# Attention stage of a ViT layer: router matmuls inside the second score train, wide weights in two buffers, q expanded by ScalarE, values split around the second heads

## The reference, cut to what matters

```python
# 64 images of 36 tokens, width 192; 12 heads of 16; 8 experts, 2 chosen; inner width 768
h = patches(x) @ W.T + b
q, k, v = split(h @ w_qkv)
a = softmax((q @ k.T * SCALE) * (1 - temperature * eye(n)))
h = layernorm(h + (a @ v) @ w_proj + b_proj)
scores = sqrt(softplus(h @ gate_w))               # router, top 2 of scores + gate_bias
expert = lambda x, W1, W2, W3: (silu(min(x @ W1, 10)) * clip(x @ W3, -10, 10)) @ W2
h = layernorm(h + expert(h, w1s, w2s, w3s) + sum over the two chosen e of weight_e * expert(h, w1[e], w2[e], w3[e]))
```

## Time and profile before

| | |
|---|---|
| median of 3 runs | 707.46 us (705.86 to 707.53) |
| profiled execution | 701.57 us, of which the span shown is 699.8 us |
| mean granted TensorE clock | 0.897 of full speed |
| PE busy | 607.3 us (87%) |
| DVE, ACT, POOL busy | 467.0, 330.9, 209.1 us |
| first group's scores read by DVE | at 30.78 us |
| last group's | at 246.79 us |

### The profile page before, as it was taken

How to read it: one execution, slowest core, us unless ns; L and a number is a source line. 1 busy time by engine, 2 the same in 40 slices (tenths; PEclk the granted TensorE clock), 3 DMA queues, 4 the chain that set the end, 5 groups by cost and what they waited for, 6 DMA issues and landing times.

```text
span 699.8 us, 15524 instructions
## 1 busy us (share of the span) xinstructions
PE 607.3 (87%) x4542; PEld 468.0 (67%) x4543; DVE 467.0 (67%) x1072; ACT 330.9 (47%) x596; POOL 209.1 (30%) x215
## 2 busy tenths in 40 slices
PE   4979999998999978884278999999999999999981
PEld 2767778686787866553146777777777777777761
DVE  0376887878768795772358766666666666667785
ACT  1456654656637553741123444444444444445434
POOL 1123444243433442337720022222222212122232
PEclk9999988799959756997569999999999999999995
DMA  7152534435350532522210111111111111111612
GB/s 273 57 175 65 163 94 142 137 99 162 117 163 14 163 97 48 166 60 77 71 46 19 24 40 40 40 40 40 40 39 37 35 39 36 40 40 39 206 32 101
DMA packets 56680, 57.97 MB, mean 83 GB/s; under 512 B 22817, under 2 KB 52785, under 8 KB 55377
## 3 DMA queue, kind: packets, MB, share of 16 engines
q1 hardware_dynamic: 52752, 49.63, 24.3%
q0 software_dynamic: 3904, 8.06, 3.4%
HBM read 41.83 MB, written 15.83 MB: 82 GB/s over the span
## 4 chain that ended last, share of the span: by engine, by line
PE 69%; DVE 12%; issue 6%; another core or an unknown queue 5%; ACT 4%; POOL 1%; DMA 1%; ACTq 0%; SPq 0%; DVEq 0%; POOLq 0%
PE bank L679 25%; PE bank L700 12%; PE bank L689 6%; PE bank L540 6%; PE bank L525 4%; PE bank L551 3%; PE bank L598 3%; PE bank L610 2%; PE bank L580 2%; PE bank L667 2%; PE bank L563 1%; DMA con<-consts 1%; PE bank L613 1%; DVE arena L980 1%
## 5 line engine op out<-in xcount | busy, mean ns | idle before, releaser
L679 PE MATMUL bank<-W,arena 128*128 (+1 forms) x1220 | 214.1, 331 | 6.2 <-issue 6.2
L679 PEld LDWEIGHTS bank<-W,arena 128*128 128x128 f16 x1220 | 121.1, 99 | 82.1 <-issue 12.3
L700 PE MATMUL bank<-W,arena 128*128 (+1 forms) x1098 | 106.9, 254 | 20.9 <-issue 11.7
L700 PEld LDWEIGHTS bank<-W,arena 128*128 128x128 f16 x1098 | 96.6, 101 | 31.0 <-issue 13.2
L1509 POOL DMA_INDIRECT ybuf<-arena,slot x43 | 41.9, 974 | 217.9 <-ACT arena L898 213.1
L1183 DVE SCALAR_TENSOR_TENSOR arena<-bank,sct,arena 128x384 f16<-128x384 f32 x86 | 49.1, 613 | 73.1 <-ACT arena L890 73.1
L525 PE MATMUL bank<-arena,par 128*96 128x288 f32 x192 | 64.0, 427 | 10.5 <-DMA con<-consts 10.0
L1197 DVE SCALAR_TENSOR_TENSOR arena<-arena 128x384 f32<-128x384 f32 x122 | 69.4, 569 | 4.2
L689 PE MATMUL bank<-con,arena 128*128 128x128 f32 x366 | 55.8, 288 | 17.1 <-issue 14.4
L884 ACT ACTIVATE arena<-bank,sct 128x384 f32<-128x384 f32 x86 | 50.0, 581 | 42.9 <-PE bank L679 41.6
L1192 DVE TENSOR_SCALAR arena<-bank,sct 128x384 f32<-128x384 f32 x86 | 58.2, 677 | 9.1 <-PE bank L679 8.9
(11 more groups left out here) (156 smaller groups left out, 898.5 us busy)
## 6 DMA issues: line engine op xcount, KB each, us to landing
stage<-w_all SPq DMA_DIRECT2D x9, 1344.0 KB, 6.0
arena<-xT SPq DMA_DIRECT2D x8, 864.0 KB, 4.6
stage<-w_all SPq DMA_DIRECT2D x9, 768.0 KB, 5.0
arena<-dbuf SPq DMA_DIRECT2D x43, 96.0 KB
dbuf<-arena SPq DMA_DIRECT2D x6, 679.0 KB, 7.1
W<-ybuf SPq DMA_DIRECT2D x3, 1152.0 KB, 8.2
xbuf<-arena SPq DMA_DIRECT2D x8, 216.0 KB, 2.3
arena<-xbuf SPq DMA_DIRECT2D x3, 576.0 KB, 5.8
```

What stands on the lines that cost most here:

```text
L679: m = pe.matmul(bank[2 * k + n][:, 0:I // 2], xT16[:, b, lo, tail, :], W16[:, bass.ds(off + at + col, I // 2)], start=(z == 0), stop=(z == ...
L700: m = pe.matmul(bank[6][:, 0:C], hhT[:, lo, ic, :], W16[:, bass.ds(off + at + ic * C, C)], start=(ic == 0 and z == 0), stop=(ic == IC - 1 ...
```

## The change

- PE: the three router tiles, two matmuls each, stand after the 4th, 5th and 7th score matmul of the second train; their logits lie in another PSUM bank, so the wait for `s_lgr` moves from ahead of `probsT(g, 0)` to ahead of `heads(g, 0)`. `project(g+1, 1)` moves ahead of `probsT(g, 1)`. The values are split: one half ahead of `heads(g, 1)`, the other behind.
- ACT: q is expanded by six ACT instructions, not two of DVE. `h1T_out` and the first half of `hT_out` stand ahead of the first exponential; the tail's `weights_hi` stands ahead of the second.
- DVE: it normalises the second half itself, behind its own `sums`. `weights_lo_tail` is moved ahead of nine steps of the choice, `weights_lo_main` behind the second `heads_out`.
- SP: `main` goes in turn to `stage` and to the unused part of `W16` that later holds the last expert; it is loaded two groups ahead, the tail one group ahead.

```diff
+        mains = stage[:, MAIN:STW], W16[:, E * WF:(E + 1) * WF].bitcast(F32)[:, 0:UPW + DNW]
+        logits = bank[4][0:TM, 440:440 + GTILES * E]
+        ROUTER_AFTER = (4, 5, 7)
...
                 wait_apart(sp, s_wlo, g * 2 + 1)
-                load_main(g + 1)
-                if tail:
+                load_tail(g + 1)
+                if main:
                     wait_apart(sp, s_wlo, g * 2 + 2)
-                    load_tail(g + 1)
+                    load_main(g + 2, odd)
...
+                        if routing and n in ROUTER_AFTER:
+                            router_tile(g - 1, ROUTER_AFTER.index(n), logits, g * 2 + 1)
...
-                scores(g, 1, None if last else embed(g + 1, 1))
-                if not start:
-                    router(g - 1)
-                    pe.wait_ge(s_lgr, g)
+                scores(g, 1, None if last else embed(g + 1, 1), routing=not start)
                 probsT(g, 0)
                 if not last:
                     project(g + 1, 0)
                 heads(g, 0)
+                if not last:
+                    project(g + 1, 1)
                 probsT(g, 1)
                 if not last:
-                    project(g + 1, 1)
+                    values(g + 1, (0,))
                 heads(g, 1)
                 if not last:
-                    values(g + 1)
+                    values(g + 1, (1,))
...
+            def q_out(g):
+                for tp in range(2):
+                    act.wait_ge(s_qk, g * 4 + 1 + tp)
+                    for hh in range(HH):
+                        m = AC.activation(qblk[:, tp].rearrange("p b (h n) -> p h b n", h=HH)[:, hh],
+                                          bank[tp][0:RT, 0:GT].rearrange("p (b n) -> p b n", b=G), ACT.Copy,
+                                          scale=K("qmask")[0:RT, hh:hh + 1])
+                    m.then_inc(s_q, 1)
...
                 if not start:
                     h1T_out(g - 1)
-                weights_hi(g, (0,))
                 if not last:
-                    hT_out(g + 1)
+                    hT_out(g + 1, (0,))
+                exps(g, 0)
+                weights_hi(g, odd, (0,))
+                if not last:
+                    hT_out(g + 1, (1,))
                 if not start:
                     logits_out(g - 1)
+                weights_hi(g, odd, (1,))
                 exps(g, 1)
                 probsT_out(g, 0)
+                if not last:
+                    q_out(g + 1)
                 if not start:
                     softplus_ln(g - 1)
-                weights_hi(g, (1,))
                 probsT_out(g, 1)
...
                 sums(g, 1)
-                weights_lo_main(g)
-                between(2)
+                normalise(g, 1)
                 heads_out(g, 0)
-                between()
-                if not last:
-                    q_out(g + 1)
-                between(2)
                 weights_lo_tail(g)
-                between(4)
+                between(9)
                 heads_out(g, 1)
+                weights_lo_main(g, odd)
                 if last:
                     x_lo(0, 0)
                 norm(g, between)
...
                 if i == COUNT_AT + 2:
-                    weights_lo_main(E)
+                    weights_lo_tail(E)
                 elif i == COUNT_AT + 3:
-                    weights_lo_tail(E)
+                    weights_lo_main(E, 0)
```

More of the change, by code:

```diff
@@ L446, in _ @@
             load_x(XT, 1)
-            group(GROUPS - 1, load=False, store=False, choice=False, tail=False)
+            group(GROUPS - 1, 1, load=False, store=False, choice=False, main=False)
             def load_h1(q):
@@ L542, in project, with values @@
                     m.then_inc(s_qk, 1)
-            def values(g):
-                pe.wait_ge(s_q, g * 2 + 2)
-                for half in range(2):
+            def values(g, halves=(0, 1)):
+                if 0 in halves:
+                    pe.wait_ge(s_q, g * 2 + 2)
+                for half in halves:
                     for pair in range(2):
@@ L761, in _ @@
             X(1, 1)
-            router(GROUPS - 1, 4)
+            for t in range(GTILES):
+                router_tile(GROUPS - 1, t, logits_last, None)
             pe.wait_ge(s_lgr, GROUPS)
```

144 lines of the change are left out of this document (77 added, 67 removed).

## The result

| us | before | after |
|---|---|---|
| median of 4 runs | 706.66 (703.14 to 707.53) | 686.80 (685.51 to 688.14) |
| profiled execution | 701.57 | 688.09 |
| its span | 699.8 | 686.3 |

The ratio is 0.9717 (95% interval 0.9662 to 0.9773): faster by 19.9 us, where 8.2 were forecast. 686.8 lies 12.5 under the forecast and 0.2 under its range.

The account below looks back on a forecast made before the run. PE, busy 87% of the span, was taken as the bound. Groups -23.3, last group +3.0, after them +1.2, falls +10.9 took 701.57 to 693.4 profiled; 5.9 more for the median gave 699.3 us, range 687 to 712.

Parts of the forecast that it names:

- the term +10.9: Seven groups: the clock falls in three of them, each costing 3.6 us, adding 10.9 us to the forecast.
- Forecast 27.6: Length of one group at full clock; six of these and a first of 27.1 make 192.7 against 216.0 us.
- The walk: One group of the new order followed engine by engine at full clock, from its first score matmul to the next group.
- the 0.45 us by which DVE was to be late: Next group's mask on DVE: comes at 5.45 instead of 5.0, since the wide low half makes norm start later.
- rival (e): Wait ahead of heads: moved, not removed, 1.5 us from the narrow high half; longer ACT work gives 705 us; chance 0.11.
- +3.0: Last group: proj waits for x_lo behind the wide low half on DVE; between +2.6 and +3.8 us, taken as +3.0.
- +1.2, +-2: After the groups: last expert's later low half is the wide one, +1.2 us; instruction arrival during dispatch -2 to +2.
- the 5.9: Level: median of before's runs stands 5.9 us above its profiled execution, added to turn 693.4 into 699.3.
- (b): Clock in the groups: no or hardly any fall, 688.4 us; chance 0.24.
- (a): Clock in the groups: falls in some, three of seven taken, 699.3 us, own range 693 to 706; chance 0.40.
- (c): Clock at the wait ahead of the first heads: falls in every group as before, slower, 713.9 us; chance 0.19.
- (d): Groups: POOL's power holds up DVE's wide low half by 2.4 us in six groups, 713 us; chance 0.06.

Follow-up runs that it names:

- b_filler: Kernel before with five unread 200-column matmuls on constants ahead of the wait for the logits, in all groups but the last; median 692.41 us of four runs.
- b_plain: Kernel before with plain stores to fixed places for the 36 indirect scatters, so its result is not the reference's; median 674.48 us.
- a_plain: Changed kernel with plain stores to fixed places for the 36 indirect scatters, so where rows go is left out; median 650.76 us.
- best1: Changed kernel with x_lo ahead of the last group's wide low half and ACT's narrow high half behind the first probabilities; 688.92 us, ratio 0.9695 to before.
- a_third: Changed kernel unchanged, run again in the fourth job beside before; median 665.92 us of six, ratio 0.9743 to before.
- b_again: Kernel before unchanged, run again in the second job; median 685.25 us of twelve.
- b_third: Kernel before unchanged, run again in the fourth job; median 683.52 us of 11.
- b_router_train: Kernel before with only the router moved into the second score train, with the logits bank, wait and h1T copies this needs; median 692.72 us, ratio 1.0114.
- a_router_back: Changed kernel with the router matmuls behind the second score train again and the logits wait ahead of the transposes; median 686.78 us of ten.

## Why the forecast missed

**What the clock costs: the step that failed.** Of the errors that put the forecast too high the largest is in the term +10.9, three falls at 3.6 us each. The price was taken from "PE is busy in the whole of the first three rows, so each us at 1.2 GHz costs half a us": 58 us, 29 us lost, 4.1 a fall, less 0.5. PE is busy there, but the group isn't longer by half of it. In the old order a group without a fall has two waits of PE further on, 1.63 us ahead of the second transposes and 1.47 ahead of proj (b_filler). A fall of 3.4 us makes PE 1.7 late and takes the place of one of them: of the first in the earlier trace rows, a group with such a fall, where q took 3.70 us and the second transposes at 73.07 waited for nothing; of the second in b_filler. Timeline of PE, before:

```profile
68.01 3.70 PE L540 MATMUL bank<-arena,par 96*112 96x288 f32 x8
```

The table's profiles give the groups two to six of the old order 29.7 without a fall (b_filler alone has any), 29.7 to 29.8 with one of 3.4 us, 31.5 with two, the second of which begins at proj, 31.2 with one of 10.2 us that begins behind the first transposes and 32.9 behind the second, and 34.4 with 17.1. The first group of before pays for its fall, which begins behind the longer wait: it takes 29.06, where b_plain, whose fall lies ahead of that wait, takes 27.51 (timeline of PE, before with its fall from 43.9, then b_plain with its fall from 38.3):

```profile
43.35 1.17 PE L580 MATMUL bank<-con,arena 108*128 108x108 f32 x8 [2.32 <-POOL arena L1442]
```

```profile
43.97 0.93 PE L580 MATMUL bank<-con,arena 108*128 108x108 f32 x8 [0.62 <-POOL arena L1442]
```

The seventh takes 29.19 in b_filler. So the seven groups of before without falls would be about 27.5 + 5 x 29.7 + 29.2 = 205.2 us, an estimate, and some 11 us of the 216.0 were lost, not 29: I had taken waits that hide a fall for time that the fall had cost.

In the new order that cover is gone: 26.85 without a fall, 28.5 with 3.4 us of it (half of it, in full), 30.2 with 6.8. There the rule of the half holds, and what the term had wrong is the length: I took the old mean, 58 us in seven falls, where only the shortest kind came. Two of 1.7 make 3.4 us, in place of 10.9. This is 7.5 us of the miss. The number of falls, three, was near; in seven profiles of after's order in the groups it was none to three. Why they are shorter than in the old order is not shown.

**The length of a group.** Forecast 27.6, measured 26.85; for seven groups without falls 192.7 against 187.0 (a_plain), 5.7 us of the miss. The walk was right in each wait: none ahead of the transposes, 1.65 forecast and 1.19 to 1.25 measured ahead of the heads, 0.5 and 0.48 ahead of proj. The 0.75 are small things with one sign: ACT's three logits instructions and the hT copy overlap (the narrow high half ended at 13.3 on the walk's scale, not 13.9), and the 0.45 us by which DVE was to be late did not show: the mask's idle time ahead of it ended with PE's score. The wait ahead of the heads is not ACT's load, as rival (e) and the walk had it: best1 shows that without the narrow half the second exponential only waits for DVE's subtraction. The walk was right in the wait and wrong in its cause.

**What the parts are worth.** At full clock the new order takes 2.9 us less a group than the old. Taken out of it one by one, q on ACT is worth 1.8 (28.64 against 26.85), the wide low half behind the second heads out some 2.7 (29.6 by the estimate above; 31.3 with its falls) and the split of the values 0.1. The router in the train makes a group longer, by 0.3 here (26.57 without it) and by 1.0 when it is the only change to the old order (30.76 against 29.7). These don't add up, since each depends on what else stands on the way to proj. Not tried alone: DVE's own multiply of the second half, k ahead of the second transposes, the wide weights in two buffers.

**The last group** was forecast at +3.0 and is +2.9. **After the groups** I gave +1.2, +-2; the first pair shows +9.9. For the dispatch, +2.7, the same kernels on chips B and C show +0.2 and +0.5, so there it isn't the change; on chip A this is open. Behind the tables +7.2, +3.4 and +7.8 in the three pairs, and +0.3 with plain stores; part of it are the multiplies beside POOL's adds, 2.4 to 2.9 us in after and a_third, 1.2 to 1.5 in before, b_again and b_third. That isn't the order's doing alone: b_filler, b_router_train and b_plain, in the old order, have 2.2 to 3.0 too. What decides how they meet, and what the rest is, is not shown.

**The base.** In the profiled execution the forecast was 693.4 and 688.1 came: 5.3 off, since the two errors of the groups (13.2, and 0.7 ahead of them and in the last group) and that after them (9.9 against 1.2, 8.7) have opposite signs. The other 7.2 come from the level: I added the 5.9 by which before's runs stood above its profiled one; after's median stands 1.3 under its own. Those 5.9 were no constant; before's 24 runs in the first job of experiments go from 682 to 720 us. So the 12.5 us are smaller than their parts: had the time after the groups been forecast right, the miss would have been some 21.

**The rivals.** (b), hardly any fall, 688.4, is nearest in the number and by luck: two falls came, and the seven groups alone gave -25.7 where it had -23.3, with +9.9 after them where it had +1.2. (a) had the number of falls, not their price. (c) did not come: falls in two groups of seven. (d) is refuted: 3.01 beside a power of 4.19. The Trainium skill, page "SBUF — State Buffer", section "SBUF: two separate sides", would have the low half wait until the power is done; the trace disagrees for the power and agrees for POOL's adds, beside which DVE's multiply took 2.52 in place of 0.56.

## What to carry to other kernels

Price lost clock by the distance of like stages with and without a fall, not by half of the slow time: where the engine waits later in the same stage, the fall is paid from that wait, and it becomes dear only when the wait is removed. Walk one stage engine by engine at full clock for both orders, and forecast a change by the two walks' difference and the falls by themselves; here the first is some -18 (187.0 against about 205.2) and the second some -7 of the -25.7. Don't carry the offset between one profiled execution and the median over to a changed kernel, and compare versions only within one job on one chip.

## What the hardware showed that I had not expected

- Falls begin behind short waits of PE, but not behind each. Behind the old order's 1.5 us between router matmuls and transposes one began in six groups of six (before). Behind the 1.19 to 1.35 us ahead of the first heads in the new order it was 14 of 42 groups in seven profiles, each time 1.4 to 2.1 us after the wait had ended. Behind 0.80 to 0.91 us that follow matmuls of 8 columns it was four of six, once for 10 us (a_router_back). Behind 2.90 us ahead of the second transposes it was all six (b_router_train).
- The same program took 706.7, 698.7, 685.2, 709.1 and 683.5 us in five jobs; after beside it 19.9, 21.8 and 17.6 us less in three of them. The 698.7 and 709.1 are of the same chip.
- The plain stores in place of the scatters shortened what comes behind the tables by 9 to 15 us (b_again and b_plain 347.7 to 338.2, after on chips B and C 351.1 and 353.2 to 338.5 and 338.2), though they were done long before; whether it is where the routed rows lie in DRAM was not tried.
